# Zero paddings spread over the routed steps, and halves of the activation first: one core, attention into routed feed-forward

## The reference

```python
x = x + tanh(g_xattn[0]) * xattn(layernorm(x), ctx, pos, pos, Wq, Wkv, Wout, bout)
x = x + tanh(g_ffn[0]) * ffn(layernorm(x), gate_w, w1, w2, shared_w1, shared_w2)
...
# xattn: 32 heads of 16, axial rotary positions, softmax over 128 context rows, out projection
# ffn:
shared_out = silu_and_mul(xf @ shared_w1.T) @ shared_w2.T
probs = softmax(xf @ gate_w.T)
routing_weights, selected = top_k(probs, 6)            # of 16 experts, width 352
moe_out = einsum('te,tei,ehi->th', combine, silu_and_mul(einsum('th,eoh->teo', xf, w1)), w2)
return moe_out + shared_out
```

## Time and profile before

| | us |
|---|---|
| median of 3 runs (range) | 1402.27 (1402.11 to 1406.74) |
| the profiled execution's own time | 1402.34 |
| its span, first to last instruction | 1400.5 |
| TensorE busy in the span | 1327.6 (95%) |
| VectorE, GpSimd, ScalarE busy | 771.1, 698.2, 570.2 |
| granted TensorE clock, mean of the span | 0.979 |

### The profile page before, as it was taken

How to read it: one execution, slowest core, us unless ns; L and a number is a source line. 1 busy time by engine, 2 the same in 40 slices (tenths; PEclk the granted TensorE clock), 3 DMA queues, 4 the chain that set the end, 5 groups by cost and what they waited for, 6 DMA issues and landing times.

```text
span 1400.5 us, 32702 instructions
## 1 busy us (share of the span) xinstructions
PE 1327.6 (95%) x8414; PEld 1136.8 (81%) x8415; DVE 771.1 (55%) x1572; ACT 570.2 (41%) x1374; POOL 698.2 (50%) x968
## 2 busy tenths in 40 slices
PE   3799999999998988999999999999999999999998
PEld 2567766766765777999999999999899999998887
DVE  3467777777776743444444444444544444446776
ACT  3567767767666412323233332333233332321121
POOL 4344554554545743388343455555533450186673
PEclk9799999999998899999999999999999999999999
DMA  5022332332323665443444445444444443267885
GB/s 201 13 91 105 115 128 80 121 119 80 128 94 130 222 218 170 145 150 111 122 145 146 149 143 153 146 144 127 124 126 146 149 143 90 87 169 223 268 248 157
DMA packets 152395, 196.93 MB, mean 141 GB/s; under 512 B 33155, under 2 KB 103300, under 8 KB 149524
## 3 DMA queue, kind: packets, MB, share of 16 engines
q1 hardware_dynamic: 130292, 104.03, 24.6%
q0 software_dynamic: 22048, 92.23, 19.5%
HBM read 122.11 MB, written 74.07 MB: 140 GB/s over the span
## 4 chain that ended last, share of the span: by engine, by line
PE 75%; DVE 9%; ACT 6%; issue 5%; SPq 3%; DMA 1%; ACTq 0%; DVEq 0%; POOL 0%; POOLq 0%
PE bank L1556 35%; PE bank L1601 19%; PE bank L712 5%; ACT soft L598 4%; PE bank L737 4%; PE bank L1568 3%; PE bank L719 3%; PE bank L751 2%; DVE smax L1012 2%; PE bank L824 2%; PE bank L768 1%; DVE x L1057 1%; DVE attn L1051 1%; DVE stats L1060 1%; ACT at_hi L623 1%
## 5 line engine op out<-in xcount | busy, mean ns | idle before, releaser
L1556 PE MATMUL bank<-w_hi,x_hi 128*128 (+1 forms) x1144 | 289.4, 334 | 0.0
L1556 PE MATMUL bank<-w_hi,x_lo 128*128 (+1 forms) x1144 | 276.8, 323 | 0.0
L1556 PE MATMUL bank<-w_lo,x_hi 128*128 (+1 forms) x1144 | 276.7, 323 | 0.0
L211 POOL CAST w_hi<-w_raw 128x352 fp32r<-128x352 f32 x152 | 72.9, 529 | 372.7 <-PE bank L1556 372.7
L1498 ACT ACTIVATE silu<-bank 128x352 f32<-128x352 f32 x143 | 66.5, 465 | 424.1 <-PE bank L1556 424.0
L1672 DVE SCALAR_TENSOR_TENSOR act<-silu,row_w,bank 128x352 f32<-128x352 f32 x111 | 64.4, 581 | 300.9 <-ACT silu L1498 300.5
L1556 PEld LDWEIGHTS bank<-w_lo,x_hi 128*128 128x128 f32 x1144 | 198.9, 188 | 0.0
L1556 PEld LDWEIGHTS bank<-w_hi,x_lo 128*128 128x128 f32 x1144 | 198.7, 188 | 0.0
L1556 PEld LDWEIGHTS bank<-w_hi,x_hi 128*128 128x128 f32 x1144 | 192.0, 189 | 0.6 <-issue 0.6
L1601 PE MATMUL bank<-w_hi,a_hi 128*128 (+3 forms) x429 | 171.1, 399 | 17.0 <-DVE a_lo L1655 14.6
L598 ACT ACTIVATE soft<-bank,smax 128x128 f32<-128x128 f32 x512 | 147.3, 381 | 81.9 <-DVE smax L1012 81.9
(11 more groups left out here) (186 smaller groups left out, 2165.5 us busy)
## 6 DMA issues: line engine op xcount, KB each, us to landing
xr<-expert_rows SPq DMA_DIRECT2D x444, 64.0 KB
y_rows<-y SPq DMA_DIRECT2D x111, 256.0 KB, 2.1
w_raw<-in_w POOLq DMA_DIRECT2D x19, 1408.0 KB, 6.7
w_raw<-in_w POOLq DMA_DIRECT2D x19, 512.0 KB, 7.8
xr<-x_rows SPq DMA_DIRECT2D x88, 64.0 KB
x_t<-x_rows SPq DMA_DIRECT2D x22, 256.0 KB, 4.1
x_sb<-in_x SPq DMA_DIRECT2D x16, 256.0 KB, 3.8
x_res<-in_x SPq DMA_DIRECT2D x16, 256.0 KB, 3.0
```

The costliest lines, as they stand in the source:

```text
L211: nc.gpsimd.tensor_copy(w1_hi[d][half][:, s], w1_raw[:, d, halves[half]]).then_inc(w_hi_made, 1)
L1556: last = nc.tensor.matmul(to[:, 0:WIDTH], xx[jt][:, d, :], w[d][half][:, cols], start=(d == 0 and xx is x_hi and w is w1_hi), stop=(d == D ...
```

## The change

Three edits, and the length of the written-out part that they need:

1. SyncE writes 4 paddings before it sends the table off and 2 more before it reads it back (before: 8 and 2). The other ten stand one in each of steps 3 to 12, behind that step's load (before: two in each of steps 4, 5, 6, ahead of its store and load). The two fixed ones move from step 7 to step 13, and the waits for paddings to steps 7, 11 and 15.
2. In steps 4 to 15 ScalarE does `a_high(i-1)` ahead of `x_high(i+1)`, and VectorE `a_low(i-1)` ahead of `turn_x(i+1)`. Steps 3 to 15 are written out, and the loop starts at step 16.
3. In the last round of attend `x_high` of tile 0 moves from group 2 to group 1 on ScalarE, and `x_low` of tile 0 from group 3 to group 2 on VectorE.

```diff
+FIRST_PADS = 6
...
-                        first_pads(range(0, 8))
+                        first_pads(range(0, 4))
                         sp.wait_ge(table_done, 1)
                         sp.dma_start(table_dram, table_p[0:BLOCKS, :]).then_inc(table_out, 16)
-                        first_pads(range(8, 10))
+                        first_pads(range(4, 6))
...
-                        if u == 2:
+                        if u == 1:
                             x_high(0, 0, 0, 0)
...
-                        if u == 3:
+                        if u == 2:
                             x_low(0, 0, 0)
...
-        LOOP_FROM, LOOP_TO = EARLY + 4, (ROUTED_END - 4) // 2 * 2
+        LOOP_FROM, LOOP_TO = EARLY + EXPERTS - 6, (ROUTED_END - 4) // 2 * 2
...
+        def halves_first(i):
+
+            return i is not None and 3 < i < LOOP_FROM
...
-                if i is not None and EARLY - 2 <= i < EARLY + 1:
-                    if i == EARLY - 2:
-                        sp.wait_ge(pad_zero, 1)
-                    k = i - EARLY + 2
-                    pads(range(10 + 2 * k, 12 + 2 * k))
-                if i == EARLY + 1:
-                    sp.wait_ge(pads_out[1], 16 * 4)
-                    sp.wait_ge(pads_out[2], 16 * 4)
-                    dump_pads()
-                if i == EARLY + 3:
-                    sp.wait_ge(pads_out[0], 16 * 6)
-                    sp.wait_ge(pads_out[3], 16 * 4)
+                m = None if i is None else i - (EARLY - 3)
+                if m is not None and m % 4 == 0 and 4 <= m < EXPERTS:
+                    sp.wait_ge(pads_out[m // 4], 16 * 4)
...
+                if m is not None and FIRST_PADS + m < EXPERTS:
+                    if m == 0:
+                        sp.wait_ge(pad_zero, 1)
+                    pads(range(FIRST_PADS + m, FIRST_PADS + m + 1))
+                if m == EXPERTS - FIRST_PADS:
+                    dump_pads()
+                if m == EXPERTS - 4:
+                    sp.wait_ge(pads_out[0], 16 * 6)
...
+                    if halves_first(i):
+                        a_high(*at(-1))
                     x_high(t, j, n, before)
                 if live(i, -2) and routed(i, -2):
                     y_out_of_psum(*at(-2))
-                if live(i, -1):
+                if live(i, -1) and not halves_first(i):
                     a_high(*at(-1))
...
+                if halves_first(i):
+                    a_low(*at(-1))
                 if starts_tile(i, 1) and i != 3:
                     turn_x(*tile(i, at, 1))
...
-                if live(i, -1) and i != 3:
+                if live(i, -1) and i != 3 and not halves_first(i):
                     a_low(*at(-1))
```

## The result

The changed kernel takes 1396.51 us (median of 8 executions, 1393.67 to 1399.27); the kernel before took 1403.28 beside it (8, 1400.88 to 1406.74). The ratio is 0.9948 with a 95% interval of 0.9934 to 0.9963: faster by 0.5%, some 7 us, where 13.7 were forecast, and 1.5 us above the upper end of the stated range (1395). The profiled execution took 1397.16, 5.2 less than the one before, and its span is 1395.0.

What follows compares the result with a forecast made beforehand. TensorE, busy 95% of the span, was taken as the bound, with idle time at three places. Gains of 2.8 (Place A), 7.4 (Place B) and 3.5 (place C) sum to 13.7, from 1402.34 to 1388.6 us; range 1381 to 1395.

Steps and rivals of the forecast that it cites:

- Place B: 506.55 to 517.27 us: down(4) waits 6.38 us for a_lo behind late tile 6's turn; gain 7.4, ends 5 and 8.3.
- place C: 540.77 to 549.66 us: down(8) waits 4.39 us for a_lo behind late tile 10's turn; gain 3.5, ends 1 and 6.9.
- Place A: Last attention round, 446.6 to 450.2 us: TensorE waits 3.59 us for ScalarE's exponentials; gain 2.8, ends 0 and 6.
- Rival 1: Place A gives nothing: a small operation of the chain is held to the subtractions' end; 1391.4 us, chance 0.15.
- rival 4: Steps 4 to 15: VectorE becomes the bound, x_lo of 5.09 costing 3.5 a step; 1402 to 1416 us, chance 0.02.
- The page's rule: VectorE instructions with two SBUF inputs and GpSimd's SBUF reads contend, the second blocking; Place A gains 1.4, sum 12.3.
- The single paddings, costed at nothing: Ten single paddings cost TensorE nothing while SyncE keeps half a us per step; otherwise each up to 1.4 us.

Runs made afterwards that it cites:

- version 3: The kernel before with only the paddings edit, steps 3 to 15 written out: 1395.16 us, ratio 0.9935.
- version 4: The kernel before with only a_hi and a_lo first in steps 4 to 15, paddings as before: 1401.94 us, ratio 0.9996.
- version 2: The changed kernel with the move of tile 0's x_high and x_low undone: 1395.12 us, ratio 0.9940 to the kernel before.
- Version 5: version 2 with ScalarE's y of step i-2 ahead of a_hi and x_hi in steps 4 to 15: 1392.37 us, ratio 0.9919 to the kernel before.
- Version 9: version 7 without paddings in steps 5 and 6, later ones two steps later, fixed ones in step 14: 1384.78 us, ratio 0.9857 to the kernel before.
- version 7: The changed kernel with GpSimd waiting for tile 0's x_lo and y first in steps 4 to 15: 1388.43 us, ratio 0.9895 to the kernel before.
- version 6: The changed kernel with GpSimd's clearing and split waiting for tile 0's x_lo: 1390.34 us, ratio 0.9910 to the kernel before.
- version 12: The kernel before with only tile 0's x_hi and x_lo earlier and GpSimd's split waiting for that x_lo: 1397.53 us, ratio 0.9969.
- version 14: Version 5 with tile 0's x_lo in group 4 and GpSimd's clearing and split behind group 2's smax: 1385.58 us, ratio 0.9866 to the kernel before.

## Why the prediction was wrong, and where it was right

**Place B, right.** Forecast 7.4, found 7.73. The table's last operation to the read: SyncE was waiting for the table this time, as said (the write went out 0.03 us after the table's end); down(4) followed up(5) at once; the wait that is left, 0.58, is for act behind the turn, with a VectorE x_lo of 0.94. Versions 3 and 4 split it: paddings alone 4.9, halves alone 4.3, both 7.7, since they partly cover the same wait. That the whole kernel keeps nothing of edit 2's part (versions 2 and 3) is the fault of place C.

**Place A, wrong in sign.** The step that failed: "x_lo moves to about 436.3 ... GpSimd is then in its casts ... Beside such casts x_lo took 0.81 ... so I cost it at nothing." The row from 556.99 was sound, and the 225 x_lo of the routed steps in all fourteen traces that started inside casts bear it out: median 0.80, none over 1.2 us. But it was a row of another GpSimd run, one that had begun after a wait of 22.70. The nearest row was x_lo at the very same place, 5.09, and the question to ask of it was not how long but until when: it was held until the run's end (445.90, x_lo ended at 446.44). Moved earlier, it waits longer for the same end. I had looked at what it was beside and not at what it waited for. Rival 1 had the mechanism (an operation held to the end of the subtractions), but on the chain, and with nothing rather than a loss as its price; rival 4 had x_lo's hold as a loss, but in steps 4 to 15. The loss at A with its sign was missing. So A is 7.9 us short of the forecast in the traces and C 3.4 short; 1.6 of A's is the scatter between steps 0 and 1. That the time still fell is B, and is not owed to edit 3, which alone makes the kernel slower.

The Trainium skill, "SBUF — State Buffer", section "Who interferes with whom", was weighed in the prediction as well: two such instructions contend, the second waits for the first. In the routed steps the traces mostly agree: of 191 x_lo that started 4.6 to 4.8 us into eight subtractions 181 took 1.25 to 1.38, about their 0.69 and the rest of the one subtraction under way. At place A they do not: it waited for 7 casts and 8 subtractions. The page's rule alone would have made edit 3 harmless, as my sum did.

**Place C, right in the load, wrong in the sum.** Tile 10's turn came 25.7 us after up(6), forecast 25.5. The step that failed: "act(9) and the transposes come 3.3 later: up(10) at 538.7". That took down(8) to be done before the turn, since its a_lo was. It also needs the bank of y(7), and y stands behind x_hi on ScalarE, so down(8) started 2.1 us after the turn and then ran in 4.00 at the slow clock instead of 2.1: up(10) started 6.6 after the turn (537.59 to 544.18), where the sum had 3.3 and 0.5 for the clock. That is 2.8 of the 3.5 that C was to give. Version 5 showed it by taking only y out of the way (2.9 us). The rest is the load: with the fixed paddings out of its way it was to land about 1 us sooner than in its 9.8 of before, and it took 10.7. In costing a move I had followed the two operations that the edit moves, and not the third that it leaves behind the same wait.

**The single paddings, costed at nothing.** The step that failed: "The ten single paddings cost TensorE nothing as long as that holds: their cover is SyncE's half us per step." Loads did gain on TensorE, but at place C it is a load that bounds, so what stands ahead of it on SyncE is not covered. Version 9 takes two paddings from there and is 3.7 us below version 7 in the medians, which is about what it gains from step 5 to step 9 (29.01 less 26.18) and a part of their scatter.

## What to carry to other kernels

When an instruction is far longer in one place than elsewhere, find the event at which it ends before moving it: if that is the end of another engine's run, moving it earlier buys a longer wait, and what stands behind it on its engine waits too. When operations are reordered so that a late input hurts less, list everything that the same step's consumer needs, result banks included; the one left behind the late input takes over the whole wait. And an issue that is covered in most steps is not covered in front of the one load that bounds: there each small thing that the queue does first counts in full.

## What the runs showed of the hardware

A run of GpSimd instructions without a gap can hold a VectorE instruction, and all behind it, to the run's end. At place A, in all nine kernels where the run followed on the last indirect scatter without a gap, the first x_lo or prob that met the run was held so (x_lo for 4.28 to 10.26 us, or prob for 4.69), whatever its size. In the five where GpSimd stood still for 1.7 us or more before the run (versions 6, 7, 9, 12 and 14) none was, though prob, pick and row lay in the same subtractions. When in the run the operation came does not sort them: held ones started from 2.6 us ahead of the first subtraction to 3.4 into them, free ones 0.3 to 5.1 into them. So at place A the standstill decides, as far as one trace of each kernel shows; left open is only a first operation that comes late in such a run, since prob, the first of the free ones, always came 0.3 to 0.9 us into the subtractions. Whether it matters that the scatter is an indirect DMA, or only that nothing lies between, no run here separates.

In the routed steps, where each run begins after a wait, it happens too, but seldom: of 475 x_lo that started inside a subtraction between 500 and 1300 us, in fourteen traces, 10 took 4.77 to 4.86 us and the others at most 1.9. The one in the trace of before, on GpSimd and on VectorE:

```profile
996.87 7.29 POOL L215 TENSOR_TENSOR w_lo<-w_raw,w_hi 128x352 fp32r<-128x352 f32 x8
1004.11 1.72 POOL L223 CAST w_hi<-w_raw 128x512 fp32r<-128x512 f32 x3
1005.91 2.85 POOL L226 TENSOR_TENSOR w_lo<-w_raw,w_hi 128x512 fp32r<-128x512 f32 x2
```

```profile
1001.52 4.86 DVE L1651 TENSOR_TENSOR x_lo<-x_t,x_hi 128x512 fp32r<-128x512 f32 x1
```

It ended at 1006.38, 0.47 after the only gap in the run (from 1005.83 to 1005.91). It started 4.65 us into the subtractions; others in the same trace that started 4.63 to 4.66 into theirs took 1.34 to 1.38. So the start alone doesn't decide whether the turn is got. What does is open.
